# Inverse roots by a power on Pool instead of eight steps on VectorE, with a new order of the stages

## The reference

```python
q = _l2norm(split(x_tri @ Wq)); k = _l2norm(split(x_tri @ Wk)); v = split(x_tri @ Wv)
attn = softmax(einsum('bnhdm,bnhem->bnhde', q, k) * rescale)
...
h1 = gelu(depthwise3x3(gelu(conv1x1(x_dct)))); x_conv = h1 + x_dct
x_high = gelu(conv1x1(x_conv)) + x_conv
x_out = coef * x_low + (1 - coef) * x_high + x_dct      # then inverse DCT, residual: x1
...
t = _ln_t(tokens(x1))                                   # and again inside the experts:
xn = (t - mean(t)) * rsqrt(var(t) + 1e-5)
y = sum over the two best experts e of weight_e * (gelu((xn * ln_g_e + ln_b_e) @ W1_e + b1_e) @ W2_e + b2_e)
```

## Time and profile before

| | |
|---|---|
| median of 3 runs | 231.08 us (228.62, 231.86, 231.08) |
| the profiled execution | 230.22 us, of which the span from first to last instruction is 228.0 us |
| mean granted clock of PE | 0.978 of full speed |
| busy | PE 199.9 us (88%), DVE 131.4 (58%), ACT 127.3 (56%), POOL 51.9 (23%) |
| the expert part from 128.8 us on | 99.2 us |

### The profile page before, as it was taken

One profiled execution on the slowest core, in us unless ns is written; L12 is line 12 of the kernel. 1 busy time (PEld: TensorE's weight loads), 2 busy tenths in 40 slices (PEclk: granted clock), 3 DMA queues, 4 the chain that ended last, 5 costly groups with the idle time before them and its releaser, 6 DMA issues.

```text
span 228.0 us, 6079 instructions
## 1 busy us (share of the span) xinstructions
PE 199.9 (88%) x2674; PEld 105.6 (46%) x2674; DVE 131.4 (58%) x231; ACT 127.3 (56%) x207; POOL 51.9 (23%) x54
## 2 busy tenths in 40 slices
PE   6868797999928977839689999999999999999992
PEld 2544486773404557737134344444444444444430
DVE  0597047909996998699981633554333554334554
ACT  2337942230072955546967587666687666786630
POOL 5380096019109996030120000000000000000000
PEclk9979999999997999997999999999999999999999
DMA  6990000000000000000004954360805406062001
GB/s 203 282 267 12 0 6 3 4 3 3 0 0 3 1 3 3 3 3 6 0 0 150 228 116 88 73 157 3 184 0 125 108 19 167 3 157 73 3 0 46
DMA packets 6601, 14.27 MB, mean 63 GB/s; under 512 B 2736, under 2 KB 4144, under 8 KB 5680
## 3 DMA queue, kind: packets, MB, share of 16 engines
q1 hardware_dynamic: 6576, 13.89, 24.8%
HBM read 12.71 MB, written 1.18 MB: 61 GB/s over the span
## 4 chain that ended last, share of the span: by engine, by line
PE 58%; DVE 26%; ACT 6%; DMA 5%; issue 3%; SPq 1%; DVEq 0%
PE psum L730 22%; PE psum L712 20%; PE psum L555 3%; DMA wide<-gate_store 2%; DMA xs<-in_x 2%; PE psum L529 2%; DVE place L1063 2%; PE psum L565 1%; PE psum L515 1%; DVE row L1062 1%; DVE place L1059 1%; DVE place L1007 1%; DVE place L1112 1%; DVE st L1106 1%; DVE st L1003 1%
## 5 line engine op out<-in xcount | busy, mean ns | idle before, releaser
L712 PE MATMUL psum<-tok,w1s 128*64 128x512 f16 x512 | 60.3, 382 | 2.0 <-ACT w1f L881 1.2
L1186 DVE SCALAR_TENSOR_TENSOR term<-psum,sm,wide 128x512 f32<-128x512 f32 x32 | 24.0, 751 | 59.1 <-PE psum L730 51.6
L881 ACT ACTIVATE hid<-psum,b1p 128x512 f32<-128x512 f32 x64 | 38.2, 700 | 15.5 <-PE psum L712 15.2
L712 PEld LDWEIGHTS psum<-tok,w1s 128*64 128x64 f16 x512 | 28.8, 111 | 35.5 <-issue 8.9
L730 PE MATMUL psum<-hid,w 128*64 128x512 f32 x128 | 28.9, 593 | 0.0
L881 ACT ACTIVATE w1f<-psum,b1p 128x512 f32<-128x512 f32 x32 | 19.5, 687 | 15.5 <-PE psum L712 15.4
L1191 DVE TENSOR_TENSOR x<-x,term 128x512 f32<-128x512 f32 x32 | 22.1, 692 | 1.1
L881 ACT ACTIVATE w1g<-psum,b1p 128x512 f32<-128x512 f32 x32 | 19.6, 712 | 0.3 <-PE psum L712 0.3
L730 PEld LDWEIGHTS psum<-hid,w 128*64 128x64 f32 x128 | 9.1, 137 | 15.0 <-issue 9.7
L555 PE MATMUL psum<-h_pad,tap_bd 64*64 64x512 f32 x144 | 16.0, 590 | 0.0
L730 PE MATMUL psum<-w1g,w 128*64 128x512 f32 x64 | 15.1, 594 | 0.1
(11 more groups left out here) (147 smaller groups left out, 289.9 us busy)
## 6 DMA issues: line engine op xcount, KB each, us to landing
wide<-gate_store SPq DMA_DIRECT2D x14, 512.0 KB, 6.3
xs<-in_x SPq DMA_DIRECT2D x2, 512.0 KB, 4.6
w1f<-in_W SPq DMA_DIRECT2D x2, 512.0 KB, 9.2
block_out<-x SPq DMA_DIRECT2D x4, 256.0 KB, 6.5
wide<-gate_store SPq DMA_DIRECT2D x2, 384.0 KB, 5.0
hid<-in_W1T SPq DMA_DIRECT2D x1, 512.0 KB, 10.2
w<-in_W SPq DMA_DIRECT2D x1, 512.0 KB, 12.3
sm<-in_small SPq DMA_DIRECT2D x1, 407.0 KB, 6.6
```

The costliest lines, as they stand in the source:

```text
L712: mm = pe.matmul(h_bank(tile)[side * H:(side + 1) * H, :], w1s[:, part, e, k * P + side * H:k * P + (side + 1) * H], tok[:, pair, half, b, :],
L881: act.activation(hid_of[u % 4][:, B2 * k + b, :], h_bank(tile), ACT.Gelu, bias=b1p[:, e * KT + k:e * KT + k + 1]).then_inc(gelu_ready, 1)
L1186: dve.scalar_tensor_tensor(term[:, u % 2, :], y_bank(u), b2t[:, e:e + 1], gate_b[part][:, e % (E // 2), :], ALU.add, ALU.mult).then_inc(te ...
```

## The change

The inverse roots become one instruction each on POOL: a tensor with itself as base and a tensor of -0.5 as exponent, `ALU.pow`. `inverse_norms` ends with its maximum; `root_of_norms` on POOL makes the roots; the new `spread_roots` on DVE holds what came behind them. `norm_tokens` ends with the variances; `root_of_tokens` on POOL makes the roots; the new `scale_tokens` on DVE scales. The inverse root of the columns at the start (`norm_columns`) stays as it is. The table TURN is written anew, with one entry of UPS and two of GELUS.

```diff
-    "norms": (16, 20), "mask_gram": (5, 7), "taps": (19, 22), "logits": (18, 23), "products": (6, 9),
-    "keep_tk": (13, 14), "inverse_norms": (8, 11), "scale_logits": (10, 14), "norms_of_k": (21, 25),
+    "norms": (16, 20), "mask_gram": (3, 5), "taps": (19, 22), "logits": (18, 23), "products": (4, 8),
+    "keep_tk": (13, 14), "inverse_norms": (6, 11), "scale_logits": (10, 15), "norms_of_k": (21, 25),
...
-UPS = (45, 47, 48, 49, 50, 51, 52, 55)
+UPS = (45, 47, 48, 49, 50, 51, 52, 54)
-GELUS = (33, 34, 35, 36, 38, 39, 42, 44)
+GELUS = (33, 34, 35, 36, 37, 39, 42, 46)
...
+            pool.memset(minus_half[:, :], -0.5)
...
+            def root_of_norms(p):
+
+                pool.wait_ge(norms_read, p + 1)
+                r = root[:, p]
+                pool.tensor_tensor(r[:, 1, :], r[:, 3, :], minus_half[:, :], ALU.pow).then_inc(norm_roots, 1)
+
+            def root_of_tokens(p):
+
+                pool.wait_ge(vars_ready, p + 1)
+                two = lambda a: st[:, p, a:a + 2, :].rearrange("p a g -> p (a g)")
+                pool.tensor_tensor(two(4), two(2), minus_half[:, 0:2 * G], ALU.pow).then_inc(token_roots, 1)
...
-                dve.wait_ge(norms_read, p + 1)
-                inverse_root(r[:, 1, :], r[:, 3, :], r[:, 2, :])
+
+            def spread_roots(p):
+
+                r = root[:, p]
+                dve.wait_ge(norm_roots, p + 1)
...
-                count(dve.tensor_scalar(s[:, 2, :], s[:, 0, :], 1.0 / H, LN_EPS, ALU.mult, ALU.add))
-                link(dve.tensor_scalar(s[:, 3, :], s[:, 0, :], (1.0 + LN_EPS) / H, LN_EPS ** 2, ALU.mult, ALU.add))
-                two = lambda a: s[:, a:a + 2, :].rearrange("p a g -> p (a g)")
-                inverse_root(two(4), two(2), two(6))
+                dve.tensor_scalar(s[:, 2, :], s[:, 0, :], 1.0 / H, LN_EPS, ALU.mult, ALU.add)
+                dve.tensor_scalar(s[:, 3, :], s[:, 0, :], (1.0 + LN_EPS) / H, LN_EPS ** 2, ALU.mult, ALU.add).then_inc(vars_ready, 1)
+
+            def scale_tokens(p):
+
+                s = st[:, p]
+                dve.wait_ge(token_roots, p + 1)
```

More of the change, by code:

```diff
@@ L48 @@
-    "norms": (16, 20), "mask_gram": (5, 7), "taps": (19, 22), "logits": (18, 23), "products": (6, 9),
-    "keep_tk": (13, 14), "inverse_norms": (8, 11), "scale_logits": (10, 14), "norms_of_k": (21, 25),
-    "softmax_in": (12, 15), "softmax_out": (13, 17), "gelu_depthwise": (15, 17), "gelu_out": (18, 22),
+    "join": (4, 6), "rest_ahead": (5, 8), "high": (7, 9), "gram_matrices": (12, 15), "gram_times_w": (14, 17),
+    "norms": (16, 20), "mask_gram": (3, 5), "taps": (19, 22), "logits": (18, 23), "products": (4, 8),
@@ L51 @@
+    "keep_tk": (13, 14), "inverse_norms": (6, 11), "scale_logits": (10, 15), "norms_of_k": (21, 25),
+    "softmax_in": (12, 17), "softmax_out": (13, 19), "gelu_depthwise": (15, 17), "gelu_out": (18, 22),
     "conv_out": (24, 29), "project": (26, 31), "exponent": (16, 21), "heads": (27, 32), "times_wv": (28, 33),
-    "keep_y": (19, 23), "low": (30, 35), "mask_mix": (16, 19), "keep_yt": (20, 24), "to_frequencies": (34, 38),
-    "inverse_over_kh": (36, 41), "keep_back": (25, 27), "keep_half": (26, 29), "square_tokens": (28, 32),
@@ L54 @@
[L54 to L57, removed]
+    "keep_y": (19, 23), "low": (30, 35), "mask_mix": (18, 21), "keep_yt": (20, 24), "to_frequencies": (34, 38),
+    "inverse_over_kh": (36, 40), "keep_back": (25, 27), "keep_half": (26, 29), "square_tokens": (28, 32),
@@ L58 @@
+    "mix_branches": (20, 22), "inverse_over_kw": (37, 42), "high_part": (30, 38), "tokens": (39, 44),
+    "residual": (23, 26), "norm_tokens": (24, 28), "keep_tokens": (31, 45), "features": (43, 53), "low_part": (12, 14),
+    "router": (41, 46), "route": (27, 30), "gates_to_rows": (55, 56), "shares": (31, 32), "biases": (7, 16),
+    "tanh_gap": (40, 41), "keep_gates": (43, 44),
 }
@@ L259, in metaformer @@
         root = sb("root", [P, PAIRS, 4, 2 * G * HEADS])
+        minus_half = sb("minus_half", [P, P])
         row = sb("row", [P, PAIRS, 3, HEADS * G])
@@ L961, in weights_of_first @@
                 pool.tensor_tensor(w1s[:, 1, :, :], w1g[:, :, :], w1s[:, 0, :, :], ALU.subtract).then_inc(w1_ready, 1)
-            for stage, (p,) in in_turn((weights_of_first, join, rest_ahead, high, low_part)):
+            for stage, (p,) in in_turn((weights_of_first, join, rest_ahead, high, low_part, root_of_norms, root_of_tokens)):
                 stage(p)
@@ L1193, in _ @@
             stages = (norm_columns, mask_gram, products, inverse_norms, scale_logits, softmax_in, softmax_out, mask_mix, mix_branches,
-                      residual, norm_tokens, route, biases, shares)
+                      residual, norm_tokens, scale_tokens, spread_roots, route, biases, shares)
             for stage, args in in_turn(stages, early(ADDS, add_expert) + late(experts)):
```

5 lines of the change are left out of this document (3 added, 2 removed).

## The result

The changed kernel is slower: 261.31 us (median of three, 260.75 to 263.01) against 231.08, a ratio of 1.136 with a 95% interval of 1.124 to 1.148. The profiled execution took 261.31 us, span 259.5: 31.5 us more than before.

A forecast was written before the change was run, and what follows sets the result against it. Bound: TensorE and VectorE at different times, a DVE, ACT, PE chain through pair 1's root, then token norms and routing. -2.3 - 0.9 + 0.3 = -2.9 us, so 228.2 against 231.08 (227 to 229.5; outer range 225.0 to 232.6).

The forecast's parts named there:

- The price of a power: Pool's power, estimated as eight passes in one instruction: 2.4 us for 128 columns, 0.7 for the token norms' 32.
- its own signs of being wrong: Prediction called wrong if powers last over 5.5 us, or TensorE's taps or Pool's high become what is last.
- rival 3: Slow power, 10 us: norms(1) late, second power holds the port, token roots lose 1.0 per pair; 239 us, chance 0.12.
- The walk through the order: New order followed with old durations up to softmax_in(1): start at 68.0 or 70.1 instead of 71.40, middle gain 2.3 us.
- parts 1 and 2: Norm roots on Pool: pair 0 costs nothing, covered up to a power of 5.5 us; pair 1 gains 2.3 us.
- rival 1: Power as cheap as a product, 0.4 and 0.2 us: softmax_in(1) 4.1 us sooner, tokens gain 1.4; 225.9 us, chance 0.25.
- the count of collisions in softmax(0): Before norms_of_k(1): softmax(0) steps on VectorE wait for Pool, so norms_of_k(1) starts at 64.5 or 66.7 instead of 68.02.
- The port: SBUF port shared by Pool and VectorE: the biases, with two SBUF inputs, wait for pair 0's whole power.
- the cover of the first power: Pair 0: products(1) ends before norms(1) starts at 48.80 for powers up to 5.5 us; beyond, every microsecond counts.
- So that is free: join(0) behind the second power in Pool's queue, 53.9 instead of 50.27: free, as only conv_out(0) at 61.58 waits.
- Part 3: Token roots, between second variance step and scaling: 0.9 us gained of 1.83; pair 1's saving doesn't reach the end.
- Part 4: End of the prologue: an up goes ahead of the gates' transposes on TensorE, first gates 0.3 us later.

The follow-up runs named there:

- six products: Changed kernel with six linked plain products for each norm power and four for each token power, roots left out: 224.29 us, 0.981 of the kernel before.
- one product: Changed kernel with a single plain product in place of each power, roots left out: 225.24 us, 0.980 of the kernel before.
- the probe: Kernel before plus a row of Pool products and powers at its end, beside the experts' additions on VectorE; executed once, no kernel time given.
- half of the columns: Changed kernel with norm powers on 64 of 128 columns, products on the others and for the tokens: 231.09 us, 1.012 of the kernel before.
- the order alone: Changed kernel's new order, with all roots by eight steps on VectorE instead of powers: 240.58 us, 1.046 of the kernel before.
- a quarter of the columns: Changed kernel with norm powers on 32 of 128 columns, products on the others and for the tokens: 225.21 us, 0.978 of the kernel before.
- eleven operations: Changed kernel with norm roots in eleven linked plain operations on Pool, token roots back on VectorE: 227.06 us, 0.986 of the kernel before.
- root in PSUM: Kernel before in its old order, root of pair 1 on VectorE with operands in PSUM, nine steps: 223.84 us, 0.973 of the kernel before.

## Why the prediction was wrong

**The price of a power** is the step that failed. I had no row of one and worked it out from passes over the columns: 2.4 us for the norms and 0.7 for the tokens, as many passes as the root has steps. It is 21.2 and 5.44. The prediction had named its own signs of being wrong, powers over 5.5 us and Pool's high as what is last, and both came. "Nothing in the trace excludes 10" was the right sentence, and 10 was still half of it; an end of 10 was itself a guess, and rival 3 deserved more than 0.12.

**The walk through the order** (parts 1 and 2) had the direction and, for rival 1, the size: 0.980 measured, 0.978 forecast. At the forecast's own price six products gave 0.981 (0.972 to 0.990) where 0.988 was forecast: inside the interval, so the time alone doesn't show the walk to be off. The rows do, and the step is the count of collisions in softmax(0): I had four of its steps wait for Pool, one did, and the spread of pair 1 began 23.2 us after the maximum of pair 0 (59.24 - 36.04) instead of 25.6. softmax_in(1) came 5.6 us sooner than before, by that distance, and not 2.3. Rival 1's time was met, its middle stage was not: with one product the spread of pair 1 met join(1) (3.37 us) and norms_of_k(1) took 3.56, so that softmax_in(1) was 1.7 us sooner where it had 4.1. That profiled execution took 227.69 us, 2.4 above its kernel's median, so its middle stage may not be that of the others.

**The port.** I let VectorE's steps with two SBUF operands wait for the whole power. They don't, which is why the cover of the first power is not 5.5 us but about 10 (11.9 us of root delayed the maximum of pair 1 by 1.5): products(1) runs beside it. The Trainium skill, SBUF — State Buffer, SBUF: two separate sides, says that of a VectorE step with two SBUF inputs and a Pool step that reads SBUF, whichever starts first has the shared port pair for its whole instruction. Plain Pool steps agree here: VectorE's subtraction, with both inputs in SBUF, took 1.68 us instead of 0.69 behind a step of high that had begun first. The powers don't: the same subtraction kept 0.69 us during the second power of the changed kernel (65.70), as the 28 additions of the probe did.

**"So that is free", of join(0) behind the second power**, held against the kernel before up to a root of about 6 us, because softmax_in(1) had come sooner by more, and not beyond. I had looked for who waits for join(0) alone, and had dismissed the end of the queue ("its last step of high(1) isn't late") from the start of join(1) at T = 2.4. Behind the second root lie 30.7 us of Pool's work that end in mix_branches, and they were the path already behind a root of 3 us (six products). Rival 3 had the first half of the mechanism, norms(1) late behind the first power (the maximum of pair 1 came 24.8 us after that of pair 0, not 13.3), and for the second half named the wrong one (the port); its direction was right. At 10 us it had 6.1 us lost before the tokens, by the port, where half of the columns lost 3.6 (57.9 for 54.3), by the queue.

**Part 3** was mis-sized by the price alone: -0.9 forecast for the first pair and nothing for the second, +3.7 measured for each. **Part 4** can't be seen in the changed kernel, where TensorE waited 0.36 us for the gates (148.96). Where the tokens weren't late, it was right that TensorE goes from the last up to both transposes without a wait; the row of the six-products kernel has no idle time before it:

```profile
112.26 0.44 PE L691 MATMUL psum<-c,gates 128*128 128x128 f32 x2
```

The 0.3 us put on it wasn't measured by itself.

## What to carry to other kernels

An operation that no row of the trace shows has no price: put it into a spare stretch of the old kernel at two sizes first, which tells the time of a column and what it does to the engine beside it. When an instruction is put into an engine's queue, look at the whole queue behind it and its last consumer, not only at the next step. Where two engines hold each other up over SBUF, moving an operand to PSUM can give more than moving the work to the other engine.

## What the runs showed of the hardware

- A Pool power costs 160 ns a column and 0.3 to 0.4 us on top, whatever the number of partitions and the three values tried; a Pool product 2.28 ns a column.
- VectorE's steps with two SBUF operands kept 0.69 us beside a power (28 of 28 in the probe on the mean, and L1082 of the changed kernel), and took 0.99 to 2.21 us beside plain Pool steps (L1201 of the probe, L1082 at 92.20 in the changed kernel). A step with one SBUF operand waited too: the first of the root, 0.23 us alone, took 1.37 and 2.37 (the order alone), but 0.29 with that operand in PSUM. Why a power doesn't hold VectorE up is not shown.
- The first root on Pool took about 0.9 us longer than the second in every kernel: 21.71 and 20.78, 11.49 and 10.55, but also 3.50 and 2.59 for five plain products. So it isn't the power's own. In the changed kernel it began at 37.35 while VectorE's product of the biases, with two SBUF operands, was running to 38.41; that this is what it waits for wasn't tried.
- norms_of_k(1), where it was TensorE's first work after an idle time, took 1.96 to 1.98 us behind 0.68 to 1.54 us of idle time (a quarter of the columns, eleven operations, root in PSUM). It took 3.3 behind 4.46 and 3.78 behind 12.61 (the order alone); the granted clock was 0.50, the level of 1.2 GHz, in both (and from 75.40 to 79.18 of the order alone).
